# A shared and routed expert layer on one core: the first row pair computed block by block, constants issued by SyncE, and ACT's copies and roundings rearranged

## The reference

```python
# x: 8 rows (b) of 512 x 256, float32; cond: 8 x 8
rw = softmax(cond); w, sel = top_k(rw, 2); w = w / w.sum()      # two experts per row
moe = sum over the two experts of w * mlp(x, gate[e], up[e], down[e])
moe = moe + mlp(x, shared_gate, shared_up, shared_down)         # shared expert
# mlp(x, g, u, d) = (gelu(x @ g) * (x @ u)) @ d, inner width 1024
x = x + moe
lora = x @ As[e].T @ Bs[e].T, summed over 8 experts with weights cond[b, e]
out = x + x @ W_base.T + b_base + 2 * lora
```

## Time and profile before

| what | value |
|---|---|
| median of 3 runs | 866.4 us (864.52 to 866.47) |
| the profiled execution's own time | 865.17 us |
| its span (first to last instruction) | 863.4 us |
| PE busy | 821.3 us, 95% of the span |
| DVE, ACT, POOL busy | 563.1, 435.9, 168.4 us |
| chain that ended last | PE 78%, DVE 9%, ACT 5%, issue 4%, DMA 2% |

### The profile page before, as it was taken

One profiled execution on the slowest core, in us unless ns is written; L12 is line 12 of the kernel. 1 busy time (PEld: TensorE's weight loads), 2 busy tenths in 40 slices (PEclk: granted clock), 3 DMA queues, 4 the chain that ended last, 5 costly groups with the idle time before them and its releaser, 6 DMA issues.

```text
span 863.4 us, 11253 instructions
## 1 busy us (share of the span) xinstructions
PE 821.3 (95%) x3670; PEld 673.6 (78%) x3670; DVE 563.1 (65%) x786; ACT 435.9 (50%) x725; POOL 168.4 (20%) x139
## 2 busy tenths in 40 slices
PE   4698998999999999999999999999999999999997
PEld 3576776777778878788888878878878888887886
DVE  4577677567677567566665666666666666667654
ACT  5565566555656445454544444544544444444442
POOL 4456444545544310010010010010001001001000
PEclk9799999999999999999999999999999999999999
DMA  5310020020151162334234323334233423433100
GB/s 177 99 50 25 24 98 25 25 97 25 47 194 54 50 207 74 110 123 133 75 107 149 109 89 132 108 97 138 93 110 120 134 73 118 137 109 96 64 1 25
DMA packets 64374, 80.34 MB, mean 93 GB/s; under 512 B 4656, under 2 KB 56880, under 8 KB 64336
## 3 DMA queue, kind: packets, MB, share of 16 engines
q1 hardware_dynamic: 63696, 79.18, 28.3%
q0 software_dynamic: 496, 0.66, 0.4%
q10 hardware_dynamic: 144, 0.03, 0.0%
HBM read 67.28 MB, written 12.58 MB: 92 GB/s over the span
## 4 chain that ended last, share of the span: by engine, by line
PE 78%; DVE 9%; ACT 5%; issue 4%; DMA 2%; POOL 1%; SPq 0%; ACTq 0%; DVEq 0%; POOLq 0%
PE ps_ring L514 51%; PE ps_acc L514 27%; DVE inner_lo L922 3%; ACT inner_hi L701 2%; DMA raw<-in_L_cond_shared_up_dram 2%; DVE post L1039 1%; DVE post L1018 1%; DVE wide L922 1%; DVE post L1036 1%; DVE xc L922 1%; ACT wide L701 1%; DVE post L1154 1%; DMA xbuf<-in_x_dram 1%; ACT post L774 1%; DVE post L1028 1%
## 5 line engine op out<-in xcount | busy, mean ns | idle before, releaser
L514 PE MATMUL ps_ring<-xc,wide 128*128 128x512 f32 x2208 | 542.4, 397 | 18.3 <-ACT post L774 13.8
L514 PEld LDWEIGHTS ps_ring<-xc,wide 128*128 128x128 f32 x2208 | 418.9, 191 | 114.3 <-ACT post L774 16.6
L701 ACT CAST inner_hi<-post 128x512 fp32r<-128x512 f32 x192 | 117.7, 621 | 303.2 <-DVE post L1154 222.3
L922 DVE TENSOR_TENSOR inner_lo<-post,inner_hi 128x512 fp32r<-128x512 f32 x192 | 159.8, 839 | 94.2 <-ACT inner_hi L701 92.8
L514 PE MATMUL ps_acc<-inner_hi,wide 128*128 128x512 f32 x512 | 178.2, 391 | 6.1 <-DVE inner_lo L922 5.1
L1154 DVE SCALAR_TENSOR_TENSOR post<-post,coef_now,ps_ring 128x512 f32<-128x512 f32 x128 | 95.3, 745 | 52.2 <-PE ps_ring L514 51.3
L514 PEld LDWEIGHTS ps_acc<-inner_hi,wide 128*128 128x128 f32 x512 | 96.2, 188 | 29.2 <-DVE inner_lo L922 8.1
L493 POOL TENSOR_TENSOR post<-post 128x1024 f32<-128x1024 f32 x8 | 19.3, 2406 | 468.6 <-DMA post<-sh_scratch 461.9
L514 PE MATMUL ps_acc<-inner_lo,wide 128*128 128x512 f32 x256 | 99.8, 390 | 0.0
L875 ACT ACTIVATE post<-ps_ring 128x512 f32<-128x512 f32 x128 | 75.9, 593 | 36.1 <-PE ps_ring L514 35.4
L922 DVE TENSOR_TENSOR wide<-raw,wide 128x1024 fp32r<-128x1024 f32 (+2 forms) x74 | 64.3, 909 | 39.5 <-ACT wide L701 39.5
(11 more groups left out here) (89 smaller groups left out, 465.4 us busy)
## 6 DMA issues: line engine op xcount, KB each, us to landing
raw<-n_L_cond_skill_gate_dram SPq DMA_DIRECT2D x32, 256.0 KB, 2.9
raw<-in_L_cond_skill_up_dram SPq DMA_DIRECT2D x32, 256.0 KB, 3.5
raw<-n_L_cond_skill_down_dram SPq DMA_DIRECT2D x32, 256.0 KB, 3.8
xbuf<-n_L_cond_skill_gate_dram SPq DMA_DIRECT2D x32, 256.0 KB, 2.9
xbuf<-in_L_cond_skill_up_dram SPq DMA_DIRECT2D x32, 256.0 KB, 3.3
xbuf<-n_L_cond_skill_down_dram SPq DMA_DIRECT2D x32, 256.0 KB, 3.6
xt_scratch<-xbuf SPq DMA_DIRECT2D x8, 512.0 KB, 2.7
sh_scratch<-stage SPq DMA_DIRECT2D x8, 512.0 KB, 2.9
```

Of the source, the lines that this page charges most:

```text
L514: last = pe.matmul(dst, left_[a], right_[b], start=start and n == 0, stop=stop and n == len(PASSES) - 1, skip_group_check=adds)
L701: return nc.scalar.copy(dst, src)
L922: return V.tensor_tensor(dst, src, hi.bitcast(F32), ALU.subtract)
```

## The change

In the first row pair (q = 0) the seven-product form is dropped: each of the four output blocks of a matrix is computed directly, two products each (`output`), so 8 products or 24 matmuls a matrix. The right operand is then only the four blocks of x (B12 takes T1's place, A21 takes S1's), and ACT applies gelu straight from PSUM (`gelu_block`), DVE multiplies straight from PSUM (`mul_block`). The weights' sums S1 to S4 are made and split once the unit's products are done, for the later row pairs. The first unit is written out by itself (`first_unit`): GATE blocks of row 0, then the transposes of row 1, UP blocks of row 0, then GATE and UP of row 1.

```diff
+            def output(j, part, t, bank):
+                for c in range(HC):
+                    last = product(ring[bank][:], [left(j, hl, part, BLOCKS_A[t // 2][c]) for hl in range(2)],
+                                   [right(0, hl, BLOCKS_B[c][t % 2]) for hl in range(2)], c == 0, c == HC - 1)
+                last.then_inc(product_done, 1)
...
+                for c in range(HC):            # first_unit
+                    pe.wait_ge(left_hi, c + 1)
+                    pe.wait_ge(right_hi, c + 1)
...
+                pe.wait_ge(x_landed[1], 16)
+                for c in range(HC):
+                    turn(acc[1][c], x_nat1, c)
+                pe.wait_ge(left_ready, LEFT_BLOCKS[0])
+                output(0, UP, 0, 3)
+                output(0, UP, 2, 1)
+                pe.wait_ge(right_ready, 4)
+                pe.wait_ge(sh_gelu, 1)
+                output(0, GATE, 1, 0)
...
             pe.wait_ge(ident_ready, 1)
+            for _ in range(20):
+                pe.transpose(ring[3][:, 0:P], ident[:], ident[:])
+            pe.wait_ge(x_landed[0], 16)
```

```diff
-            load_shared(1, sh_landed[1], sh_landed[1], sh_landed[1])
+            load_gate_up(1, sh_landed[1], sh_landed[1])
+            load_down(0)
+            sp.wait_ge(turned, 2)
+            load_x(2)
+            load_down(1)
+            sp.dma_start(logits[:], cond.partition_broadcast(P)).then_inc(cond_landed, 16)
...
-            pool.dma_start(bias[:], b_base.partition_broadcast(P)).then_inc(layer1_landed, 16)
-                for e in range(E):
-                    pool.dma_start(lora_w[e * R:(e + 1) * R, :],
```

```diff
+            def sums(u, part):
+                m = matrix_no(u, part)
+                dve.wait_ge(product_done, products(u, part, 2))
+                dve.wait_ge(copied, 2 * m + 2)
+                V.tensor_tensor(v57, ring[3][:], v57, ALU.add).then_inc(v_done, 1)
+                dve.wait_ge(product_done, products(u, part, 3))
+                V.tensor_tensor(u1, ring[1][:], u1, ALU.add).then_inc(u1_done, 1)
...
-                G.tensor_tensor(v57, v57, p7, ALU.add).then_inc(v_done, 1)
-                G.tensor_tensor(i_t[3], i_t[3], g_t[3], ALU.mult).then_inc(sh_mul3, 1)
...
+                    copy_out(u, GATE)          # ACT, q > 0
+                    inner_part(u - 1, 2)
+                    inner_part(u - 1, 3)
+                    gelu_sums(u)
...
+                if q > 0:                      # ACT
+                    copy_out(u, UP)
+                inner_part(u, 0)
...
+                inner_part(u, 1)
...
+                    sums(u, UP)                # DVE, q > 0
+                    shared_mul(u, 0)
+                    off_diagonals(u, UP)
+                    shared_mul(u, 1)
+                    inner_part(u, 0)
+                    shared_mul(u, 2)
+                    inner_part(u, 1)
+                    shared_mul(u, 3)
```

More of the change, by code:

```diff
@@ new lines, in _ @@
+            sp.dma_start(bias[:], b_base.partition_broadcast(P)).then_inc(layer1_landed, 16)
+            with nc.allow_non_contiguous_dma(reason="64 scalars, each to 16 partitions"):
+                for e in range(E):
+                    sp.dma_start(lora_w[e * R:(e + 1) * R, :],
+                                 cond[:, e].partition_broadcast(R)).then_inc(lora_w_landed, 16)
+            sp.wait_ge(left_ready, LEFT_BLOCKS[1])
+            sp.wait_ge(s_made, 2)
+            sp.wait_ge(sh_dn_ready, 2)
@@ new lines, in copy_out, with gelu_sums @@
+            def copy_out(u, part):
+                m = matrix_no(u, part)
+                for n, to, bank in ((0, u1, 0), (1, v57, 2)):
+                    act.wait_ge(product_done, products(u, part, n))
+                    if n == 0 and m > 0:
+                        act.wait_ge(c_done, 2 * m)
+                        act.wait_ge(c22_done, m)
+                    nc.scalar.copy(to, ring[bank][:]).then_inc(copied, 1)
+            def gelu_sums(u):
+                m = matrix_no(u, GATE)
+                act.wait_ge(product_done, products(u, GATE, 4))
+                act.wait_ge(sh_mul, 4 * (u - 1) + 1)
+                gelu_of(g_t[0], ring[0][:]).then_inc(sh_gelu, 1)
@@ L809, in _ @@
+            gelu_block(0, 1, 0)
+            split_shared_down(0)
+            gelu_block(0, 3, 2)
+            take_xt(0, 2, acc[1][0])
+            take_xt(0, 3, acc[1][1])
+            inner_part(0, 0)
+            inner_part(0, 1)
+            split_sums(0)
+            for u in range(1, NU):
                 q, j = divmod(u, PAIRS)
                 qn = q + 1
-                if qn < Q and j in (1, 2):
-                    take_xt(qn, 0 if j == 1 else 2, ring[1])
-                copy_out(2 * u, 0, u1, 0)
@@ L841, in _ @@
+                if more and j == 3:
+                    act.wait_ge(t_made, 4 * q + 4)
+                    split_right(qn, T4, t_a)
                 if u == NU - PAIRS:
@@ L1072, in _ @@
-                if qn < Q and j in (1, 2):
-                    split_right(qn, B11 if j == 1 else B21, xt(0, j - 1), j)
-                if qn < Q and j == 3:
-                    split_right(qn, T2, t_a, 5)
-                    split_right(qn, B22, xt(1, 1), 6)
-                if u == 4:
+                more = qn < Q
+                if q > 0:
+                    sums(u, GATE)
+                    off_diagonals(u, GATE)
+                inner_part(u - 1, 2)
+                inner_part(u - 1, 3)
```

777 lines of the change are left out of this document (433 added, 344 removed).

## The result

The changed kernel takes 827.3 us (median of 4 runs, 827.07 to 827.52), the kernel before 865.5 beside it (864.29 to 866.47): ratio 0.956, 95% interval 0.954 to 0.958. The forecast was 836, with a range of 829 to 851. The sign was right and so were most of the mechanisms; the losses that I had allowed for did not come. The profiled execution took 827.11 us, its span is 824.9.

A forecast was written before the change was run, and what follows sets the result against it. PE bound the kernel, losing 29.3 us in units 0 to 3 and 13.5 in units 4 to 15. Gains of 20.9 and 9.0 took own time from 865.2 to 835.3; median 1.2 above, so 836 us, range 829 to 851.

The forecast's parts named there:

- The direct form: First row pair: 3 matmuls more in each of 8 matrices, 24 in all, 5.4 us added on PE's path.
- rival 3: Start: early transfers stay slow for a reason other than lora_w, x row 1 and pair 1 late; 843 us, chance 0.11.
- the waits for ACT's copies: GATE halves, units 4 to 15: copies stand behind four roundings; 13.5 us lost, 9.0 to be gained.
- rivals 4 and 5: DVE becomes what GATE's products wait for: 844 us, chance 0.17; POOL's sums hold DVE's two-SBUF-input operations: 878 us, chance 0.03.
- SP's new order: Start: bias and lora_w cost SP nine issues, 4.5 us, before pair 3; hidden, even with 6 us more.
- the low clock: Start of PE: 2.0 us taken for running at the low clock, between 0 and 3.1.
- handovers in units 0 to 3: PE's stalls above the ideal 62.0 us to GATE(4): 1.5 us first unit, 1.0 units 1 to 3; bounds 0 and 6.
- units 5, 9 and the joints: PE's losses above the ideal 182.4 us: 3.0 us where POOL's x sums delay DVE, 1.5 at other joints.
- Rival 7: Whole kernel: no loss is left but the clock's; 830 to 829 us, chance 0.03.
- first product at: Start of PE: first product at 7.9 us instead of 10.15, after x row 0 is turned and rounded.
- routed part: After unit 15: 572.2 us at PE's pace, unchanged, 0 gained.
- The cover that I had: DVE in units 4 to 15: 0.4 us slack before GATE's third product, 1.1 us more before PE's seventh waits.

The follow-up runs named there:

- 2b: The kernel before with only the eight lora_w issues moved from POOL to SP, behind the first two stores of x; 862.99 us, ratio 0.9967.
- 4a: The changed kernel with blocks 2 and 3 of inner rounded and split within their own unit again; 839.75 us, ratio 0.968.
- 4b: The kernel before with only the rounding and splitting of inner blocks 2 and 3 moved behind the next GATE's copies; 851.4 us, ratio 0.983.
- experiment 5: The changed kernel with unused reductions added on DVE in each unit from 4 on: four a unit 838.23 us, two a unit 829.59 us.
- Experiment 1: The changed kernel without the 20 transposes of the identity at the start; 828.37 us, ratio 0.957.
- experiment 3: The changed kernel with x row 2 loaded only behind the weights of pair 2; 837.15 us, ratio 0.967.
- 2a: The changed kernel with the eight lora_w transfers issued by POOL again, right behind the identity; 831.35 us, ratio 0.959.
- experiment 6: The changed kernel with a routed down projection held back, 827.32 us; also with a shortened start, 827.57; also with DVE's splits moved later, 822.98.
- 5b: The changed kernel with two unused reductions more on DVE in each unit from 4 on; 829.59 us, ratio 0.957.
- the last of 6: The changed kernel with held down projection, shortened start, and DVE's weight split and second-layer lo half behind the row's last inner_lo; 822.98 us, ratio 0.950.

## Why the prediction was right, and where it was wrong

**What held.** The direct form costs 24 matmuls and no waits; lora_w slowed the early transfers (rival 3 is out, by 368 GB/s in 2b); the waits for ACT's copies come from its order (4a, 4b); DVE holds PE nowhere (rivals 4 and 5 are out), and POOL holds two of its operations only in units 5 and 9; SP's new order is hidden. Pair 3 was issued at 28.9, near the forecast 29.7, and landed by 39.3, before it was needed at 43.

**What failed: the losses that I allowed for.** The sum set aside 2.0 us for the low clock, 2.5 for handovers in units 0 to 3 and 4.5 for units 5, 9 and the joints, 9.0 in all. The runs showed no wait and no low clock in any of these places. Rival 7, "no loss is left but the clock's", had a chance of 0.03, and even that kept too much. By the terms of the sum:

| term | forecast | measured | from |
|---|---|---|---|
| first product at | 7.9 | 7.0 | timeline |
| clock | 2.0 | 0 | x turned in 1.04, no low clock behind it |
| handovers, units 0 to 3 | 1.5 + 1.0 | 0.7 | 62.70 against 62.0 |
| units 5 and 9, joints | 3.0 + 1.5 | 1.0 | 183.39 against 182.4 |
| routed part | 0 | -0.4 | 571.81 against 572.22 |

That makes 0.9 + 2.0 + 1.8 + 3.5 + 0.4 = 8.6 us of span, and 836 - 827.3 = 8.7 of the medians. The middle three, 7.3 us, the clock, the handovers and the joints, are one error: I priced each uncertain spot at some part of its bound and added them, though my own walk had found no late block.

The range has the same fault. Its lower end, 829, takes the 4.5 and the 2.5 out but leaves the 2.0 for the clock in, although the prediction says itself that a warm-up that fully counts makes the time 2.0 shorter. With all three at nothing it is 827.0; 827.3 was measured. That this is so close is in part luck: the sum's last step dropped half a microsecond (835.3 + 1.2 is 836.5), and the 1.7 us by which the two stages exceed their ideals are made good by the first product and the routed part, 1.3 us.

- **Units 5 and 9** are the largest, 3.0 us. The lateness of DVE was read rightly (2.2 us, I had up to 2.6), but then charged to PE at 1.5 each, and PE lost nothing: the GATE matrices behind them take 7.48 us like the others. The cover that I had, 0.4 + 1.1 = 1.5, is too small. By experiment 5 some 0.6 us are left there on top of the lateness, 2.8 in all; elsewhere it is 1.1 to 1.2 (unit 13), 1.7 or 2.4.
- **The clock.** The Trainium skill, "TensorE: Matmul & The Clock Gate", Part 4, says that the full clock does not engage for transposes. The trace disagrees: after 20 transposes of the identity alone, those of x take 1.04 us for eight instead of 1.94. Experiment 1 shows that my price was wrong on the other side too: without the 20, the low clock costs 0.9 to 1.1 us and not 3.1. The stretch itself is as long as others (3.8 us of busy time at the low level, against 3.04 and 6.15 in the earlier trace rows and 3.6 in experiment 3), but its first half falls before gate 0 lands, where PE's pace costs nothing.
- **The first product** came 0.9 us earlier. I had it wait for x: landed at 6.17, the first half turned at the low clock by 7.2, rounded by 7.9. But PE began to turn x at 5.61 and took 0.5 us for that half, at the high clock, so that gate 0, which landed at 5.96 and which my sum does not name, became the later one (experiment 1). About half of the 0.9 is thus the clock again. x row 0 landed at 4.1 us (seen in experiment 1, where PE waits for it), before at 6.17. It isn't lora_w: with it away, 2b still had x at 6.19, and with it back on POOL 2a began to turn x at 5.84, right behind the 20 transposes. Among what 2b keeps and 2a doesn't are the other small transfers at the start, the bias on POOL and the logits on ACT. The packets of the first 7 us, of 2b and of the changed kernel:

```profile
DMA packets 676, 1.29 MB, mean 185 GB/s; under 512 B 176, under 2 KB 432, under 8 KB 676
```

```profile
DMA packets 808, 1.50 MB, mean 214 GB/s; under 512 B 52, under 2 KB 572, under 8 KB 808
```

  Neither was run apart, so the cause of the earlier landing stays open.
- **The joints.** I had kept 1.5 us of the 13.5 lost before "at the other joints" without naming one, and none showed. The waits alone could not tell how much was at stake: of their 13.8 us only 5.8 lie in units 4 to 15, where 12.5 were gained, since a listed wait is shorter than its cost and does not hold the half pace behind it.

The Trainium skill, "SBUF — State Buffer", section "SBUF: two separate sides", says that GpSimd and a VectorE operation with two SBUF inputs take turns. The 1.79 and 1.77 us in unit 5 agree again, and DVE's sums from PSUM kept 0.69 beside POOL's.

**What stays open.** The 25.6 us ahead of GATE(4) are not split in full. Taken back one at a time, the early x row 2 is worth 7.7 (experiment 3) and lora_w's place about 4 (2a); the two overlap, since what 2a loses are waits for x rows. What is left, the direct form, the 24 matmuls that it adds and the clock that no longer falls, was not run apart, as the first unit's order exists only with the direct form. So no run here shows whether the direct form itself pays for its 5.4 us of matmuls.

## What to carry to other kernels

Where a walk of the orders finds no late operation and an engine's lateness stays within the cover, put zero in the sum and the doubt in the range, and let the range's lower end be the sum with every allowance at zero; half a bound at every joint adds up to an error of its own. When a wait's releaser is named, look first at what stands ahead of it in that engine's order: moving two roundings by one matrix gave 11.6 us, two copies fewer and lighter work for POOL 0.9, and at the row's end only DVE's order, not PE's, moved the gap. Small scattered transfers of constants belong behind the large ones that the start waits for. And before pricing a slow start of an engine, look at which input lands last: here what PE did slowly before gate 0 landed cost nothing.

## What the runs showed of the hardware

- **Transposes alone raise the clock, not always at the same time.** In seven traces with 20 of them ahead, the eight of x row 0 took 1.03 to 1.04 us; in 2a they took 1.59, so there the rise came later, and with none ahead 1.94. With 12 ahead, the two kernels of experiment 6 with the same start had 1.57 and 1.97.
- **Tiny transfers slow large ones.** With eight transfers of 0.5 KB under way the rate falls, though not at once: 307 GB/s from 4 to 8 us and then 38 in the kernel before, 127 and then 180 and 50 in 2a; without them it is 306 and 325 in the changed kernel and 368 in 2b. The changed kernel shows it too: its eight are issued from 21.3 to 25.6 us and take up to 12.0 to land, and pair 3, issued from 28.9 on, hardly moves before 34. It is not needed before 43. Its rate per slice of 1.1 us, from 0 to 45 us:

```profile
GB/s 0 76 378 205 243 350 375 388 399 353 59 0 171 295 0 15 131 338 231 196 239 349 230 35 0 0 0 0 0 1 8 70 271 395 424 375 404 178 0 0
```

- **The clock can fall for the last 24 matmuls.** PE stands 2.16 us before the second layer of the last row (2.54 in the kernel before, 2b and 4b). In nine of the fourteen traces those 24 matmuls take 3.12 to 3.14 us, in five (2b, 3, 4b, 5b and the last of 6) 4.55 to 4.63, at a granted clock of 0.55 in 5b. The last matmuls of the changed kernel, and of 5b with a window of them:

```profile
818.62 3.13 PE L571 MATMUL ps_acc<-xc,sh_dn 128*128 128x256 f32 x24 [2.16 <-DVE sh_dn L1107]
```

```profile
820.47 4.58 PE L572 MATMUL ps_acc<-xc,sh_dn 128*128 128x256 f32 x24 [2.16 <-DVE sh_dn L1108]
...
822.00:824.00 2.00, 2.00 (x12) 2.00 (x12) 0.49 (x1) 0.00 (x0) 0.00 (x0) 0.55 0.00 0
```

The wait is the same in both, and what decides was not found. It explains some 1.4 us of difference between such traces.
